# One router and one plan for the last four batches, and tile 0's loads moved into the attention

## Chip, cores and metric

The kernel runs on one core of one Trainium2 chip. The metric is the device time of one execution in microseconds (us), lower is better; of several runs the median counts.

## What is computed

A decoder layer on x of 16 batches of 128 tokens and 256 channels, in fp32, with three residual steps. Cut to what matters:

```
x = x + attn(layernorm(x))        # 16 heads, latent size 72, causal softmax, then out_w (1152 x 256)
x = x + sigmoid(layernorm(x)) * wkv(ctx)     # two scans over time per channel, from ctx alone
x = x + ffn(layernorm(x))
  logits = h @ router_w.T                    # 8 experts
  (w1, e1), (w2, e2) = top two experts of each token, masked softmax gates
  out = sum over experts e of w_e * (silu(h @ w_gate[e].T) * (h @ w_up[e].T)) @ w_down[e].T
```

2048 tokens each go to two of eight experts, whose hidden size is 512.

## The kernel before

**The order.** Every engine runs its own program, and all of them walk one list of steps, ORDER, which the function schedule (L60) writes at build time. Each step has a name and arguments: S, N, T, Y are scores, softmax, transposes of the probabilities and the mix with V for one unit; O projects a quarter of a batch's z; add adds it to x; bn, agg, rs, nmb, xn, tx are layer norm and its transposes; sig, x2 the gated second step; lg, lgc, r1, r2, ra, r3, rw, r4 the router; p1, p2, p3 the plan; lw and ltk load weights and token lists, lxg gathers rows; sw, tg, up, sh, dn are one tile of the expert layer. Each engine executes its part of a step in this order, and semaphores make it wait for the others.

**Attention.** 64 units (UNITS, L32), one for a batch and four heads. From unit 40 on the units of one batch follow each other. A unit's scores stand in step n, its N in n+1, its T and Y in n+3. In each unit of the loop (L365) there are five turns at which other work is taken in. Y's copy (copy_mixed, L1358) puts the mix into ZT, and SyncE packs it into zP by four DMAs (pack_z, L739). O of a batch (project, L912) reads zP.

**The planner.** The lists in beside (L282) hold generators that emit steps. At each turn (L289) a credit of st["share"] is added and the steps spend it; rest(n) (L72) puts a list to sleep for n times st["pace"] turns; users of the PSUM bank TR keep st["gap"] turns apart (L76). Before a value is needed, finish (L303) runs the generators without limits until a condition holds. stage_e (L266) is what follows the attention for a group of four batches (NG = 4): second norm, gate, x2, store of x, third norm, store of the rows to xd in HBM, their transposes, and the router. The last group is done in two halves, batches 12 and 13, then 14 and 15, each with a router and a plan of its own.

**Router and plan.** For each token the router finds two experts (choose_first L1438, choose_second L1447), counts ranks by matmuls (ranks, L949), makes slot numbers (slots, L1463) and weights (L1476), and GpSimd scatters number and weight of each token into xs in HBM (scatter_slots, L1713; one indirect DMA per batch and choice, 32 in all). A plan (L1490 to L1535) turns the counts of each expert into a list of tiles of 256 tokens: expert and first row of each go to PI, from which SyncE reads them into registers. PHASES gives how many tiles are sure after 12, 14 and 16 batches: tiles 0 to 4 come from plan 0, tiles 5 and 6 from plan 1, tiles 7 to 22 from plan 2. So tile 5 can't be loaded before batches 12 and 13 are routed.

**Tiles.** 23 tiles (NT). For a tile SyncE loads three blocks of an expert's weights (load_w, L761, 512 KB each) into WR[j % 2] and the token list into TK (load_tk, L776, which waits for all scatters that the phase needs). GpSimd gathers the rows from xd into XG[j % 4] (gather_rows, L1723), TensorE transposes them (transpose_rows, L960). Each fp32 operand is split into a high part (ScalarE, w_hi L1166, rows_hi L1179, hidden_hi L1190) and a low part (VectorE, w_lo L1537, rows_lo L1542, hidden_lo L1554), and each product is three matmuls (mm3, L811). gate_up (L971) runs twice for a tile, down (L990) once. ScalarE weighs the result into Y, and GpSimd adds it to out in HBM by two indirect DMAs (add_out, L1737), which wait until those of the tile before have landed.

**Where the change meets.** After the last Y, finish (L386) runs what is left of plan 0; then come the token lists, the weights of tiles 0 and 1, the gathers and the splits of tile 0 (L387 to L397), all still inside the unit loop, and the projections of batch 15 after them. WR[0] lies in the arena of the scans and is free when these end; WR[1], WF, GT, SG, HF, HR and Y lie over the attention's buffers (s1, L507 to L524). The tile loop (L414) has a turn (beside_turn, L405) between any two steps, seven in a tile, and emits loads up to three tiles ahead where the plan is there.

Functions that the diff touches:

## Time and profile before

| | us |
|---|---|
| median of 3 runs | 676.19 (672.5 to 677.79) |
| the profiled execution | 672.7 |
| its span | 671.0 |
| TensorE, VectorE, ScalarE, GpSimd busy | 559.1, 425.7, 368.8, 325.0 |
| mean granted TensorE clock | 0.944 of full speed |

The span runs from the first to the last instruction on the profile; the profiled execution's own time has 1.7 us around it. Rows below are from this one execution. Times in them are microseconds from the span's start. In the timeline, merged lines of one engine may cover several instructions (xN), "idle before" is how long the engine stood and what ended it.

### The profile page before, as it was taken

The numbers are of one execution on the slowest core, as the hardware profiler recorded it, in microseconds if no ns is written. First come the engines' busy times: TensorE is split into PE (matmuls) and PEld (weight loads), VectorE is DVE, ScalarE is ACT, GpSimd is POOL, SyncE is SP. The second block draws the span as 40 slices with busy tenths as digits, with TensorE's granted clock in tenths as the row PEclk, the third lists the DMA queues.
The fourth block names the chain that finished last, engine by engine and source line by source line (L and its number), as shares of the span: only waits on it lengthen the run. The fifth ranks groups of instructions, "written<-read, shape, count | busy, mean of one in ns | idle before, by whom it ended". The sixth has DMA issues, their size and how long they took to land.

```text
span 671.0 us, 11309 instructions
## 1 busy us (share of the span) xinstructions
PE 559.1 (83%) x3775; PEld 488.3 (73%) x3775; DVE 425.7 (63%) x942; ACT 368.8 (55%) x1000; POOL 325.0 (48%) x299
## 2 busy tenths in 40 slices
PE   1997869998979998999879725767889899999990
PEld 0885757776768876778657425667889899999990
DVE  4468475565876739755754617778877577777750
ACT  5276535755658545655554213655567567766750
POOL 3274635625254275621721531145546676666543
PEclk9999879999999998999999858879899899999996
DMA  6234444463434323624312145446379788888710
GB/s 234 78 55 66 54 65 73 61 89 53 65 82 98 51 42 56 103 73 62 49 60 59 36 162 203 137 105 165 88 235 248 202 211 239 219 222 226 171 30 0
DMA packets 55757, 75.92 MB, mean 113 GB/s; under 512 B 11730, under 2 KB 45140, under 8 KB 55444
## 3 DMA queue, kind: packets, MB, share of 16 engines
q1 hardware_dynamic: 45098, 64.90, 40.3%
q0 software_dynamic: 9856, 10.28, 8.3%
q8 instruction: 30, 0.49, 0.3%
q14 instruction: 27, 0.22, 0.1%
q10 hardware_dynamic: 746, 0.02, 0.1%
HBM read 48.90 MB, written 10.40 MB: 88 GB/s over the span
## 4 chain that ended last, share of the span: by engine, by line
PE 37%; DVE 21%; issue 11%; POOL 10%; DMA 9%; ACT 8%; SPq 2%; POOLq 0%; DVEq 0%; ACTq 0%
PE P L814 16%; PE PO L814 6%; PE PO L923 5%; ACT EB L1115 3%; DMA out<-Y,TK 3%; PE P L892 3%; PE P L910 2%; DVE ZT L1363 2%; DVE small L1352 2%; DVE arena L1385 2%; POOL EB L1684 2%; DMA zP<-ZT 2%; POOL xs L1720 2%; POOL out L1744 2%; DMA cxa<-xd,TK 2%
## 5 line engine op out<-in xcount | busy, mean ns | idle before, releaser
L1684 POOL TENSOR_TENSOR EB<-EB,small 128x512 f32<-128x512 f32 x64 | 75.9, 1187 | 158.6 <-DVE small L1356 158.5
L1115 ACT ACTIVATE EB<-P,small 128x128 f32<-128x128 f32 x256 | 90.3, 365 | 112.4 <-DVE small L1352 112.3
L814 PE MATMUL P<-GT,WF 128*128 128x256 f32 x1104 | 148.4, 293 | 3.2 <-DVE GT L1262 2.5
L814 PEld LDWEIGHTS P<-GT,WF 128*128 128x128 f32 x1104 | 141.5, 200 | 3.6 <-DVE GT L1262 2.7
L1744 POOL DMA_INDIRECT out<-Y,TK x46 | 83.7, 1820 | 63.7 <-DMA out<-Y,TK 36.1
L910 PE MATMUL P<-PT,V 128*72 128x512 f32 x128 | 69.1, 623 | 17.6 <-DVE ZT L1363 13.0
L1734 POOL DMA_INDIRECT cxa<-xd,TK x46 | 52.7, 1145 | 58.3 <-DMA TK<-xs 46.1
L892 PEld LDWEIGHTS P<-KT,qT 72*128 72x128 f32 x512 | 68.7, 196 | 11.6 <-DMA qT<-qP 8.2
L892 PE MATMUL P<-KT,qT 72*128 72x128 f32 x512 | 69.7, 280 | 7.1 <-DMA qT<-qP 6.7
L923 PE MATMUL PO<-Ow,zP 128*128 128x256 f32 x288 | 74.8, 401 | 0.0
L814 PE MATMUL PO<-WF,HR 128*128 128x256 f32 x552 | 70.1, 284 | 0.0
L1363 DVE COPY ZT<-P 72x512 f32<-72x512 f32 x64 | 43.0, 672 | 42.5 <-PE P L910 39.8
L814 PEld LDWEIGHTS PO<-WF,HR 128*128 128x128 f32 x552 | 68.0, 193 | 0.0
L1262 DVE TENSOR_TENSOR WF<-arena,WF 128x1024 fp32r<-128x1024 f32 x36 | 44.1, 1224 | 35.3 <-ACT WF L1177 35.3
L923 PEld LDWEIGHTS PO<-Ow,zP 128*128 128x128 f32 x288 | 54.1, 200 | 8.6 <-issue 0.2
L900 PEld LDWEIGHTS P<-ident,EB 128*128 128x128 f32 x256 | 33.0, 146 | 37.1 <-issue 32.4
L1352 DVE TENSOR_REDUCE small<-P 128x4 f32<-128x512 f32 x64 | 43.4, 677 | 23.1 <-PE P L892 23.0
L1262 DVE TENSOR_TENSOR WF<-WR,WF 128x1024 fp32r<-128x1024 f32 x33 | 40.4, 1224 | 21.0 <-ACT WF L1177 21.0
L1120 ACT ACTIVATE PT<-P 128x512 f32<-128x512 f32 x64 | 38.6, 603 | 25.7 <-PE P L900 25.5
L1115 ACT ACTIVATION_READ_ACCUMULATOR EB<-P,small 128x1 f32 x256 | 51.9, 203 | 0.0
L1177 ACT ACTIVATE WF<-arena 128x1024 fp32r<-128x1024 f32 x36 | 38.0, 1055 | 17.8 <-DMA arena<-wf 17.8
L1720 POOL DMA_INDIRECT xs<-TKS,SL x32 | 37.9, 1184 | 20.0 <-DVE TKS L1481 12.0
(187 smaller groups left out, 945.0 us busy)
## 6 DMA issues: line engine op xcount, KB each, us to landing
arena<-wf SPq DMA_DIRECT2D x36, 512.0 KB, 4.4
WR<-wf SPq DMA_DIRECT2D x33, 512.0 KB, 4.4
qT<-qP SPq DMA_DIRECT2D x63, 128.0 KB
zP<-ZT SPq DMA_DIRECT2D x80, 72.0 KB
zP<-ZT SPq DMA_DIRECT2D x96, 36.0 KB
X<-x SPq DMA_DIRECT2D x4, 512.0 KB, 6.0
cxa<-ctxin SPq DMA_DIRECT2D x4, 512.0 KB, 6.5
out<-X SPq DMA_DIRECT2D x3, 512.0 KB, 3.8
```

What stands on the lines that cost most here:

```text
L814: r = e.matmul(o, lt(a), rt_(b), start=start and n == 0, stop=stop and n == 2, skip_group_check=skip)
L892: p = e.matmul(S[:, 128 * j:128 * j + 128], qT[k % 2][:, 4 * hq + j, c:c + 128], KT[g % 2][:, r:r + 128], start=False, stop=True, skip_gro ...
L910: e.matmul(YB[0:L, :], V[g % 2][:, b % GB, :], PT[n % 2][:, :], start=True, stop=True).then_inc(s_Y, 1)
L923: p = e.matmul(o, zP[b // NB % 2][:, m, 128 * (b % NB):128 * (b % NB) + 128], Ow[:, m, :], start=False, stop=m == NQ - 1)
L1115: e.activation(EB[i][:, j, :], S[:, 128 * j:128 * j + 128], ACT.Exp, bias=NM[i][:, j:j + 1], accum_out=SM[i][:, j:j + 1]).then_inc(s_exp, 1)
L1262: return e.tensor_tensor(o, src, hi.bitcast(fp32), ALU.subtract)
L1352: e.tensor_reduce(NM[n % 3], SB[n % 2][:, :].rearrange("p (h s) -> p h s", h=4), AX.X, ALU.max, negate=True).then_inc(s_max, 1)
L1363: e.tensor_copy(ZT[z % 2][:, :, c:c + 128], YB[0:L, :].rearrange("p (h t) -> p h t", h=4)).then_inc(s_z, 1)
L1684: e.tensor_tensor(EB[i][:, :, :], EB[i][:, :, :], SM[i].unsqueeze(2).broadcast_to([128, 4, 128]), ALU.mult).then_inc(s_prob, 1)
L1720: e.indirect_dma_start(xs, bass.IndirectOffsetOnAxis(ap=SL[:, g, c, b:b + 1], axis=0), TKS[:, g, c, b, :], None).then_inc(s_sc[g + b0 // 2 ...
L1734: e.indirect_dma_start(XG[i][:, a_, :], None, xd[0:(TN * 3 // 4, TN * 7 // 8, TN + 1)[phase(j)], :], bass.IndirectOffsetOnAxis(ap=TK[:, j, ...
L1744: e.indirect_dma_start(outr, bass.IndirectOffsetOnAxis(ap=TK[:, j, a_, 0:1].bitcast(i32), axis=0), Y[j % 2][:, a_, :], None, bounds_check= ...
```

## The change

- The last group's two halves share one router and one plan: PHASES has two entries (tiles 0 to 4 after 12 batches, 5 to 22 after 16), the router of batches 12 to 15 runs when batch 15's third norm is done, and the scatters of the last group count on one semaphore.
- From unit 52 on (LATE) the planner's share is 0.9, its pace 0.6 and the gap 3; in the tiles share, pace and gap are 3, 0.5 and 3 (before 4, 0.1, 3).
- A generator lists stands behind plan 0 and emits the weight loads of tile 0 and the first three token lists during the attention, where SyncE also packs z.
- The first half of the last group gets a list of its own that starts at unit 62.
- After the loop: gathers, splits and transposes of tile 0, weights of tile 1, up(0,0), and only then the projections of batch 15 and the last add.
- Ow, Lw and the bias rows move behind zP in SBUF and no longer lie under HR and Y; w_hi(0) waits for the queries, w_hi(1) for the mixes, where both waited for projections.
- If the plan of the next tile isn't there at the end of a tile, finish runs then, before the next tile's splits; before, it ran at the tile's start.

The diff, without the lines that only rename:

```diff
 NT = (2 * TN + NE * (TW - 1)) // TW
-PHASES = [-(-(2 * n - NE * (TW - 1)) // TW) for n in (TN * 3 // 4, TN * 7 // 8)] + [NT]
+PHASES = [-(-(2 * (TN * 3 // 4) - NE * (TW - 1)) // TW), NT]
 NX = 4
-SHARE, SHARE_TILES = 0.7, 4.0
-GAP, GAP_TILES = 5, 3
-PACE, PACE_TILES = 1.0, 0.1
+SHARE, SHARE_TILES = 0.7, 3.0
+GAP, GAP_LATE, GAP_TILES = 5, 3, 3
+PACE, PACE_TILES = 1.0, 0.5
+LATE, SHARE_LATE, PACE_LATE = 52, 0.9, 0.6
 SCANS_FROM = 0
...
         if g == NG - 1:
-            yield from plan(1 + b0 // 2)
+            yield from plan(1)
...
         yield from own(e_ln3(g, b0, nb), "norm")
-        yield from own(e_route(g, b0, nb), "route")
+        if b0 + nb == GB:
+            yield from own(e_route(g, 0, GB), "route")
...
+    def lists():
...
+        yield from rest(5)
+        for k in range(3):
+            load_w(0, k)
+        yield from rest(3)
+        for j in range(3):
+            emit("ltk", j)
...
+    waiting = []
...
+    def load_w(j, k):
+        if j < NT:
+            if phase(j) in planned:
+                emit("lw", j, k)
+            else:
+                waiting.append((j, k))
...
+    def split_w(j, k):
+        if j < NT:
+            emit("sw", j, k)
+            load_w(j + 2, k)
...
     beside = [[(0, first()), (0, stage_a(1)), (0, own(ln1_stats(2), "norm")), (0, own(ln1_stats(3), "norm")), (19, stage_a(2)), (35, stage_a(3))],
               [(27, stage_e(0, 0, GB)), (43, stage_e(1, 0, GB)),
-               (54, stage_e(2, 0, GB)), (54, plan(0)), (62, stage_e(3, 0, 2))],
-              [(NU + 4, stage_e(3, 2, 2))],
+               (54, stage_e(2, 0, GB)), (54, plan(0)), (54, lists())],
+              [(62, stage_e(3, 0, 2)), (NU + 3, stage_e(3, 2, 2))],
               [(SCANS_FROM, scans(g, k)) for g in range(NG) for k in range(2)],
...
             if b >= NB * PAIRED:
-                at_i = at + (4 + i // 2 if b < B - 1 else 3)
+                at_i = at + 4 + i // 2
             else:
...
                 at_i = at + 5 + (i // fast if b % 2 == 0 else 4 // fast + (i // 2 if b % 4 == 3 else i // fast))
-            o_steps.setdefault(at_i, []).append((b, i))
+            if b < B - 1:
+                o_steps.setdefault(at_i, []).append((b, i))
...
-    waiting = []
...
-    def load_w(j, k):
-        if j < NT:
-            if phase(j) in planned:
-                emit("lw", j, k)
-            else:
-                waiting.append((j, k))
...
-    def split_w(j, k):
-        if j < NT:
-            emit("sw", j, k)
-            load_w(j + 2, k)
...
-    for n in range(NU + 4):
+    def projections_of(b):
+        for i in range(4):
+            emit("O", b, i)
...
+    for n in range(NU + 3):
+        if n == LATE:
+            st.update(gap=GAP_LATE, share=SHARE_LATE, pace=PACE_LATE)
         if 3 <= n < NU + 3:
...
         turn(n)
-        if n == NU + 2:
-            finish(n, lambda: 0 in planned and NG - 1 in w_done)
-            for j in range(3):
-                emit("ltk", j)
-            for k in range(3):
-                load_w(0, k)
-            for k in range(3):
-                load_w(1, k)
-            for j in range(3):
-                emit("lxg", j)
-            split_w(0, 0)
-            split_w(0, 1)
-            emit("tg", 0)
+    finish(n, lambda: ("ltk", 2) in order and NG - 1 in w_done)
+    for j in range(3):
+        emit("lxg", j)
+    split_w(0, 0)
+    split_w(0, 1)
+    emit("tg", 0)
+    for k in range(3):
+        load_w(1, k)
+    emit("up", 0, 0)
+    projections_of(B - 1)
+    emit("add", NK - 1)
...
     def beside_turn(upto):
-        turn(NU + 4)
+        turn(NU + 3)
         while waiting and ready(waiting[0][0]):
...
     for j in range(NT):
-        if j + 1 < NT and not ready(j + 1):
-            finish(NU + 4, lambda: ready(j + 1))
+        due = j + 1 < NT and not ready(j + 1)
...
+        def prepare(k):
+            if not due:
+                split_w(j + 1, k)
...
         beside_turn(j + 3)
-        split_w(j + 1, 0)
-        emit("up", j, 0)
+        prepare(0)
+        if j:
+            emit("up", j, 0)
         beside_turn(j + 3)
-        if j + 1 < NT:
+        if j + 1 < NT and not due:
             emit("tg", j + 1)
         beside_turn(j + 3)
-        split_w(j + 1, 1)
+        prepare(1)
         emit("sh", j, 0)
...
         beside_turn(j + 3)
+        if due:
+            finish(NU + 3, lambda: ready(j + 1))
+            beside_turn(j + 3)
+            split_w(j + 1, 0)
+            emit("tg", j + 1)
+            split_w(j + 1, 1)
     emit("dn", NT - 1)
...
         qT = [sb(f"qT{i}", [L, H, 128 * NB], fp32, s1) for i in range(2)]
+        EB = [sb(f"EB{i}", [128, 4, 128], fp32, s1) for i in range(3)]
+        PT = [sb(f"PT{i}", [128, 512], fp32, s1) for i in range(2)]
+        ZT = [sb(f"ZT{i}", [L, 4, 128 * NB], fp32, s1) for i in range(2)]
+        maskr = sb("maskr", [128, 4, 128], f32r, s1)
+        identr = sb("identr", [128, 128], f32r, s1)
+        zP = [sb(f"zP{i}", [128, NQ, 128 * NB], fp32, s1) for i in range(2)]
         Ow = sb("Ow", [128, NQ, C], fp32, s1)
...
         onr = sb("onr", [1, 128], f32r, s1)
-        EB = [sb(f"EB{i}", [128, 4, 128], fp32, s1) for i in range(3)]
-        PT = [sb(f"PT{i}", [128, 512], fp32, s1) for i in range(2)]
-        ZT = [sb(f"ZT{i}", [L, 4, 128 * NB], fp32, s1) for i in range(2)]
-        zP = [sb(f"zP{i}", [128, NQ, 128 * NB], fp32, s1) for i in range(2)]
-        maskr = sb("maskr", [128, 4, 128], f32r, s1)
-        identr = sb("identr", [128, 128], f32r, s1)
         s1.close()
...
                 if q == 0:
-                    pe.wait_ge(s_xt3, xt_count("tx", 3, g, b0, nb, 1))
+                    pe.wait_ge(s_xt3, xt_count("tx", 3, g, 0, GB, 1) if g < NG - 1 else xt_count("tx", 3, g, 2, 2, 1))
                     tr_wait("lg", g, b0, nb, q)
...
                 ac.wait_ge(s_wf[i][k], 16 * (j // 2 + 1))
-                if j == 0 and k < 2:
+                if j == 0:
                     ac.wait_ge(s_q, total["q"])
-                elif j < 2:
-                    ac.wait_ge(s_O, 4 * B)
+                elif j == 1:
+                    ac.wait_ge(s_Y, NU)
                 elif k == 2:
```

## Rows read from the trace of the kernel before

**Rows 1.** Windows of the last units, the drain, tiles 0 to 4 and the steady tiles

```profile
core 0: us, PE busy (x) PEld busy (x) DVE busy (x) ACT busy (x) POOL busy (x), PEclk, DMA share, GB/s
330.00:383.00 53.00, 45.61 (x228) 33.76 (x228) 28.33 (x93) 23.38 (x86) 19.90 (x20) 0.90 0.18 49
383.00:398.00 15.00, 0.29 (x2) 0.02 (x1) 2.99 (x14) 0.36 (x1) 6.08 (x7) 0.64 0.29 85
398.00:473.00 75.00, 53.77 (x364) 50.83 (x365) 55.94 (x181) 39.74 (x62) 22.24 (x18) 0.85 0.55 167
...
528.00:656.00 128.00, 127.70 (x1060) 127.50 (x1058) 88.94 (x107) 86.42 (x136) 79.28 (x53) 0.99 0.72 185
```

**Rows 2.** Chain of waits: start us, us, what

```profile
388.55 0.67 SPq L748
...
399.82 6.26 PE PO L923 x18
...
592.62 0.44 PE P L968 x4
...
635.11 2.88 PE P L814 x24
```

**Rows 3.** Timeline, last units to tile 0: start us, us, engine, line, op

```profile
349.44 1.90 PE L910 MATMUL P<-PT,V 128*72 128x512 f32 x2 [3.84 <-ACT PT L1120]
...
374.02 1.04 POOL L1684 TENSOR_TENSOR EB<-EB,small 128x512 f32<-128x512 f32 x1 [2.58 <-DVE small L1356]
...
382.19 1.08 PE L910 MATMUL P<-PT,V 128*72 128x512 f32 x2 [0.69 <-ACT PT L1120]
...
385.69 0.69 DVE L1363 COPY ZT<-P 72x512 f32<-72x512 f32 x1
...
392.45 0.99 POOL L1734 DMA_INDIRECT cxa<-xd,TK  x1 [7.40 <-DMA TK<-xs]
...
397.98 1.12 PE L968 MATMUL P<-ident,cxa 128*128 128x128 f32 x4 [14.71 <-DMA cxa<-xd,TK]
...
405.72 3.22 PE L814 MATMUL P<-GT,WF 128*128 128x256 f32 x24
...
406.11 0.69 DVE L1368 TENSOR_TENSOR X<-PO,X 128x512 f32<-128x512 f32 x1 [1.03 <-PE PO L923]
```

**Rows 4.** Timeline in tiles 1 to 4: batches 12, 13 and 14, 15

```profile
421.76 0.69 PE L832 MATMUL P<-ident,XN 128*128 128x128 f32 x2 [9.53 <-ACT XN L1076]
...
427.04 0.75 DVE L1293 BATCH_NORM_STATS2 small<-X 128x6 f32<-128x256 f32 x2
...
445.83 0.17 DVE L1470 TENSOR_TENSOR small<-P,small 128x16 f32<-128x16 f32 x1
...
472.66 0.17 DVE L1470 TENSOR_TENSOR small<-P,small 128x16 f32<-128x16 f32 x1
```

**Rows 5.** Waits of TensorE from 380 to 528: us in total, times, longest

```profile
PE P L968 <- DMA cxa<-xd,TK: 19.6, 3, 14.7
...
PE P L832 <- ACT XN L1076: 13.0, 2, 9.5
```

**Rows 6.** Timeline, tiles 5, 7 and 10 transposed, and scatters between

```profile
472.65 0.60 PE L968 MATMUL P<-ident,cxa 128*128 128x128 f32 x4
...
474.88 1.00 POOL L1720 DMA_INDIRECT xs<-TKS,SL  x1 [5.20 <-DVE TKS L1481]
...
482.00 2.05 POOL L1720 DMA_INDIRECT xs<-TKS,SL  x1 [0.30 <-issue]
...
484.35 2.02 POOL L1720 DMA_INDIRECT xs<-TKS,SL  x1 [0.30 <-issue]
...
497.60 0.66 PE L968 MATMUL P<-ident,cxa 128*128 128x128 f32 x4 [2.39 <-DMA cxa<-xd,TK]
...
527.63 1.11 PE L968 MATMUL P<-ident,cxa 128*128 128x128 f32 x4 [2.45 <-DMA cxa<-xd,TK]
```

**Rows 7.** Timeline, the last matmuls

```profile
649.78 5.92 PE L814 MATMUL PO<-WF,HR 128*128 128x256 f32 x48
```

More of the change, by code:

```diff
@@ L636, in build @@
         s_xd = [sem(f"xd_stored{i}") for i in range(5)]
-        s_sc = [sem(f"slots_scattered{i}") for i in range(5)]
+        s_sc = [sem(f"slots_scattered{i}") for i in range(NG)]
         s_out = [sem(f"x2_stored{i}") for i in range(5)]
@@ L778, in load_tk @@
                 for i in range(3 + phase(j)):
-                    sp.wait_ge(s_sc[i], SCATTERS[i])
+                    sp.wait_ge(s_sc[i], SCATTERS)
                 sp.wait_ge(s_fill, 48)
@@ L801, in sync_program @@
             sp.wait_ge(s_acc, 32 * NT)
+            for i in range(NG):
+                sp.wait_ge(s_sc[i], SCATTERS)
             for i in range(5):
-                sp.wait_ge(s_sc[i], SCATTERS[i])
                 sp.wait_ge(s_out[i], 16)
@@ L1491, in plan_counts @@
                 j0, n, nf, tl, te, one, first, m, v, eid, rs, un, tmp = plan_views(i)
-                second = i == 2
+                second = i == 1
                 ve_.wait_ge(s_run, 3 + i)
@@ L1505, in plan_tiles @@
                 j0, n, nf, tl, te, one, first, m, v, eid, rs, un, tmp = plan_views(i)
-                second = i == 2
+                second = i == 1
                 cmp, jb = big[0:1, 0:n, :], jio[0:1, 0:n]
@@ L1720, in scatter_slots @@
                     e.indirect_dma_start(xs, bass.IndirectOffsetOnAxis(ap=SL[:, g, c, b:b + 1], axis=0),
-                                         TKS[:, g, c, b, :], None).then_inc(s_sc[g + b0 // 2], 16)
+                                         TKS[:, g, c, b, :], None).then_inc(s_sc[g], 16)
             def gather_rows(j):
@@ L1725, in gather_rows @@
                 po.wait_ge(s_tk[j % 4], 16 * (j // 4 + 1))
-                for d in range(3 + phase(j)):
+                for d in range(5 if phase(j) else 3):
                     po.wait_ge(s_xd[d], 16)
@@ L1733, in gather_rows @@
                 for a_ in range(2):
-                    e.indirect_dma_start(XG[i][:, a_, :], None, xd[0:(TN * 3 // 4, TN * 7 // 8, TN + 1)[phase(j)], :],
+                    e.indirect_dma_start(XG[i][:, a_, :], None, xd[0:(TN * 3 // 4, TN + 1)[phase(j)], :],
                                          bass.IndirectOffsetOnAxis(ap=TK[:, j, a_, 0:1].bitcast(i32), axis=0)).then_inc(s_xg[i], 16)
@@ L1772, in build @@
         PARTS = ((0, 1024), (1024, 2048), (2048, 3072))
-        SCATTERS = [16 * 8, 16 * 8, 16 * 8, 16 * 4, 16 * 4]
+        SCATTERS = 16 * 2 * GB
         block = ctx.enter_context(nc.Block())
```

## The prediction

> **What bounds the kernel now.** I read the table of windows first. Outside the tail it has four stretches [rows 1]. In the last attention units TensorE is busy 45.61 of 53.00 us. From 383 to 398 it is busy 0.29 of 15.00. From 398 to 473, tiles 0 to 4, it is busy 53.77 of 75.00 at a granted clock of 0.85 of full speed, while VectorE is at 55.94. From 528 on it is busy 127.70 of 128.00. So TensorE bounds the later tiles and nothing in the diff makes those cheaper: three groups of 24 matmuls at 2.88 us and four transposes at 0.44 [rows 2] make 9.08 us a tile. The time to be won lies between the last unit and about tile 10.
>
> Then I followed the chain of waits and the timeline through that stretch. At its start the last z copy ends at 386.39 behind the plan's own VectorE instructions [rows 3], its packing is issued until 389.22 [rows 2], the token list comes only then, the first gather is issued at 392.45 and lands at 397.98, where tile 0 is transposed [rows 3]. The last output projection takes 6.26 us [rows 2], x1 is added at 406.11 and up(0,0) runs from 405.72 to 408.94 [rows 3]. In the middle, TensorE stands at the normalised rows of batches 12 and 13 for 9.53 us [rows 4], and the list of waits has 13.0 us in two such waits and 19.6 us in three waits for gathered rows [rows 5]. At its end tile 7, the first of the last plan, is transposed at 497.60, and tile 10 at 527.63 [rows 6].
>
> A yardstick: from the transposes of tile j to the last matmul there are 22-j tiles and then six groups, (22-j) x 9.08 + 17.7 us. From tile 5 (472.65) this gives 644.7, and the last matmul ends at 655.70 [rows 6, 7]: 11.0 us are lost after tile 5, most of them to the second plan. The tail from there to the span's end is 15.3 us. The profiled execution took 672.7 for a span of 671.0, so 1.7 is added to a span. It is 3.5 under the median of 676.19, near the fastest of the three; I return to that at the end.
>
> **Where the order moves things.** From unit 52 on the planner gives 0.9 instead of 0.7 of credit per turn and rests 0.6 as long. Walking its turns (five per unit), group 2 has its logits in unit 59 (62 before), slots at 60, p1 and p2 at 61, p3 at the start of 62 (end of 66 before). The three weight loads of tile 0 fall in unit 63, the three token lists two turns later. Batches 12 and 13 start their second norm in unit 62 and have their third norm transposed by unit 66; all that stood in tiles 0 and 1 before. In the tile phase a tile has seven turns. Counted from the first one (share 3, pace 0.5, gap 3), batches 14 and 15 have statistics in turn 1, x2 in 4, third norm in 6 and 7, transposes in 10 and 13, logits in 16, slots in 19, scatters in 19 to 22, plan in 23 and 24, which is tile 3's third turn. So tile 5's plan stands in the order before it is due, and the forced finish is empty.
>
> **Attention's end.** The moved plan is 5.1 us of small VectorE instructions, and two passes of statistics of 3.3 us each join units 62 to 66. Where such a pass sits in a unit now, TensorE waits 3.84 us for the copied probabilities and the unit takes longer at 349.44 [rows 3]. Against it, the plan no longer holds back the last z copy (2.4 us: the mix ends at 383.27, its copy starts at 385.69). SyncE gets six loads with register reads between packings, 7.5 us of its queue (389.43 to 397), and the packings of units 60 to 63 stand behind it; TensorE has up(0,0) to run meanwhile. Bounds of the net shift of the last z copy: 2.4 earlier, 6 later. I take 1.6 later, 388.0.
>
> **Tile 0 at once.** GpSimd has nothing after the last probabilities (374.02 before, [rows 3]) but gathers, so tile 0's rows land by 384, and w_hi/w_lo(0) run in the drain. The transposes of tile 0 wait for that z copy: 388.0 + 1.1 + the split of the rows (0.6 on ScalarE, 0.7 on VectorE) = 390.4. up(0,0) takes 3.2 and hides the last packing. O of batch 15 is 6.3 at the lower clock, 18 of its matmuls at 0.35 us each [rows 2]; the clock had fallen after TensorE had stood from 383.27 on, and as that stand is now some 2 us, I take 4.8, most of the matmuls at full clock (in the windows the clock was 0.64 of full speed over that stand, [rows 1]), with 7.0 as the other bound. With 0.7 for the add and some issue time the statistics of batch 14 start at 399.7.
>
> **One router.** The second chain before went from its statistics at 427.04 to its slots at 472.66, 45.6 us; the first from the end of the add, 406.80, to 445.83, 39.0 [rows 4]. The new one has about as many turns, but half of the routing beside it is gone: one set of choices (3.1 us), slots and weights (1.5) and a plan (4.6), 9 us of VectorE in the stretch where VectorE is the fuller engine. My walk through its in-order queue with these durations (7.1 us of splits and products a tile) gives 37.5. Ends 35 and 50; I take 40, nearest to the first chain. TensorE still stops once at the transposes of the normalised rows, now those of 14 and 15. Slots start at 439.7, weights are there at 441.1.
>
> **Scatters, list, gather.** Before, the last group had four scatters left; now it has eight, with one pair of output adds between them. Four at 1.27 (0.97 and the 0.3 between), 4.3 for the adds, four at about 1.8 (between 1.27 and the 2.35 of those at 482.00 and 484.35 with the 0.3, [rows 6]) are 16.5: 441.9 to 458.4. From the last scatter's end (486.37) to the transposes of its first tile (497.60) it took 11.2. So tile 5 is transposed at 469.6, against 472.65 before. TensorE could be there at about 455: some 14 us of standing, which before were spent on tiles 5 and 6 from the middle plan.
>
> **The rest.** From 469.6 the yardstick gives 641.7. Of the 11.0 us lost after tile 5 the half that belongs to the second plan goes (tiles 5 to 22 now have one plan and two lists are fetched at once); a cold restart and late output adds remain, and 3 us are kept, with 1 and 7 as bounds. Last matmul 644.7, span 660.0, time 661.7: 11 us less than the profiled 672.7. The gain is 3 us at tile 5 and 8 behind it. As medians lie a little over a profiled execution, the forecast for the median is 662.5, 2.0% under 676.19. The other moves (buffers of the attention laid out anew, waits on counts of Y for those of O) take or add no instruction on the path and are put at nothing; the new layout is what lets O of batch 15 run behind up(0,0), and without it the add would be 3 us sooner and tile 0 later by 5.
>
> **Rivals.** (a) The chain is freer than that: with 35 us to the slots and scatters at 1.27, tile 5 comes at 463 and the time is near 655. For it: half the routing, a warm clock. Against: both chains before needed 39 and more.
> (b) All scatters are slow. A scatter lasts 0.97 us beside a quiet VectorE and 2.02 to 2.05 beside its busy spell at 482 [rows 6]. Eight of these with the adds are 22.9 instead of 16.5, so 668 to 669. The Trainium skill, SBUF — State Buffer, section "Who interferes with whom", says that a VectorE instruction with two SBUF inputs blocks a GpSimd one that reads SBUF, and whoever comes second waits. By that rule every scatter of the tile phase is at risk; the trace agrees only for some of them.
> (c) Slower: TensorE starves at tile 5. The single plan is the only source of tiles behind tile 4, and nothing covers its lateness. With the second chain's 45.6, the slow scatters and a list that lands as late as the slowest scatter's (7 us more), tile 5 comes at 399.7 + 45.6 + 2.2 + 22.9 + 18.2 = 488.6 and the time is 681. It decides from tile 5 at 484.
> (d) The head start doesn't come: VectorE and SyncE, packed denser from unit 52 on, stretch the last units by 10 us or more, and tile 0 starts hardly sooner; 672 to 676.
>
> **How the numbers follow.** The forecast 0.50, (a) 0.20, (b) 0.13, (c) 0.07, (d) 0.10. Three runs of before span 5 us, so about 1% is what a measurement tells from no change; 1% under the median is 669.4. Faster takes (a), nearly all of the forecast and half of (b): 0.74. Within 1%: the rest of (b), a little of the forecast and most of (d): 0.18. Slower: (c) and what is left, 0.08. The range leaves out (c) and the far side of (a): 648 to 674.
>
> **What would show it.** In the profile after: tile 0 transposed near 389 and not 398; the last add by 400; TensorE busy between 385 and 395; one chain of choices in the tiles; eight scatters in a row near 442 to 458; one long wait of TensorE at the transposes of tile 5, for gathered rows, about 14 us; from some 478 on no waits. It is wrong if the last z copy is past 394, if tile 5 comes later than 476 or earlier than 463, or if TensorE stands again behind tile 6.

## The result, and the profile after

| | before | after |
|---|---|---|
| median, us | 675.25 (670.41 to 682.86, 20 runs) | 669.53 (666.04 to 673.01, 20 runs) |
| ratio, 95% interval | | 0.9925 (0.9898 to 0.9951) |
| span of the profiled execution | 671.0 | 665.0 |

Faster by 0.75%, where 2.0% was forecast: the right sign, inside the range, well under half the gain. The ratio is taken over all fast runs and not from the two medians, whose quotient is 0.9915; further down, too, the two can differ by 0.2%.

The windows after, with the columns of [rows 1]:

```profile
330.00:383.00 53.00, 40.32 (x204) 30.40 (x204) 35.41 (x130) 24.62 (x94) 20.43 (x20) 0.89 0.17 48
383.00:398.00 15.00, 9.97 (x38) 6.73 (x38) 5.24 (x20) 4.84 (x8) 7.27 (x8) 0.84 0.69 214
398.00:473.00 75.00, 50.81 (x359) 48.44 (x359) 47.52 (x123) 33.39 (x51) 22.89 (x19) 0.86 0.51 134
473.00:528.00 55.00, 50.73 (x408) 50.73 (x409) 35.28 (x42) 34.71 (x55) 37.43 (x25) 0.92 0.81 217
528.00:656.00 128.00, 123.55 (x1035) 123.34 (x1033) 87.21 (x106) 84.37 (x133) 79.93 (x51) 1.00 0.70 182
```

Read the first two together. TensorE is now busy for 9.97 us between 383 and 398, where it had 0.29, but not with tile 0: that is attention, which it didn't do between 330 and 383 (40.32 busy against 45.61) while VectorE had 7 us more. The drain wasn't filled with new work; the attention slid into it.

The timeline after, at the places that the prediction named (start us, us, engine, line, operation, idle before and releaser):

```profile
378.25 0.68 DVE L1380 TENSOR_REDUCE small<-P 128x4 f32<-128x512 f32 x1
...
387.98 0.69 DVE L1391 COPY ZT<-P 72x512 f32<-72x512 f32 x1 [1.03 <-PE P L938]
393.77 0.69 DVE L1391 COPY ZT<-P 72x512 f32<-72x512 f32 x1 [5.11 <-issue]
397.09 0.69 DVE L1391 COPY ZT<-P 72x512 f32<-72x512 f32 x1 [2.62 <-DMA zP<-ZT]
...
397.92 1.08 PE L996 MATMUL P<-ident,cxa 128*128 128x128 f32 x4 [2.26 <-DVE ZT L1391]
400.70 4.36 PE L842 MATMUL P<-GT,WF 128*128 128x256 f32 x24 [1.69 <-DVE GT L1290]
...
405.41 4.15 PE L951 MATMUL PO<-Ow,zP 128*128 128x256 f32 x18
...
409.60 0.69 DVE L1396 TENSOR_TENSOR X<-PO,X 128x512 f32<-128x512 f32 x1 [3.75 <-PE PO L951]
...
448.04 0.18 DVE L1498 TENSOR_TENSOR small<-P,small 128x32 f32<-128x32 f32 x1
...
477.27 1.11 PE L996 MATMUL P<-ident,cxa 128*128 128x128 f32 x4 [15.85 <-DMA cxa<-xd,TK]
...
645.63 5.92 PE L842 MATMUL PO<-WF,HR 128*128 128x256 f32 x48
```

The last z copy ends at 397.78 (386.38 before, 388.0 forecast). Tile 0 is transposed at 397.92, in the same place as in [rows 3] but for another reason: it stood behind a gather before, and stands behind that copy now. The last add comes at 409.60, 3.5 us later than in [rows 3].

TensorE's waits after, from 380 to 528 (total, times, longest):

```profile
PE P L996 <- DMA cxa<-xd,TK: 15.9, 1, 15.9
PE P L842 <- DVE GT L1290: 6.0, 2, 4.4
PE P L860 <- ACT XN L1104: 5.1, 1, 5.1
PE PO L949 <- DMA zP<-ZT: 3.1, 1, 3.1
PE P L938 <- DVE ZT L1391: 2.8, 1, 2.8
```

Beside [rows 5]: one long wait for gathered rows where there were three, and 5.1 us of waiting for normalised rows where there were 13.0. From 478 on the list of waits is empty. New are the waits for zP and ZT, which belong to the attention's end.

SyncE's own queue after, from 377 on (start, us from first to last issue, count):

```profile
377.90 2.82 SPq L775 DMA_DIRECT2D zP<-ZT  x4
382.10 2.67 SPq L801 DMA_DIRECT2D arena<-wf  x3
385.68 2.55 SPq L811 DMA_DIRECT2D TK<-xs  x3
388.27 2.92 SPq L775 DMA_DIRECT2D zP<-ZT  x4
...
391.74 2.85 SPq L775 DMA_DIRECT2D zP<-ZT  x4
...
395.14 5.85 SPq L775 DMA_DIRECT2D zP<-ZT  x8
```

The six loads stand between 382.10 and 388.23. The z copy that ended at 382.77 is packed only from 388.27, and a z copy needs the packing of the copy two before it to have landed. So the z copies at 393.77 and 397.09 stand 5.11 and 2.62 us; the profile names the releaser (<-DMA zP<-ZT) for the second and writes "issue" at the first.

### The profile page after: what moved, and what is told of

Its sections match the earlier page's. It is cut to its first block, busy times and chain, and to the rows that moved or that the text cites. A ratio compares the mean times of both kernels' runs of the same rounds, so it can differ in the third digit from the quotient of the medians.

```text
span 665.0 us, 11259 instructions
## 1 busy us (share of the span) xinstructions
PE 558.7 (84%) x3778; PEld 489.2 (74%) x3778; DVE 418.1 (63%) x888; ACT 366.6 (55%) x997; POOL 328.6 (49%) x300
## 3 DMA queue, kind: packets, MB, share of 16 engines
q1 hardware_dynamic: 45098, 64.90, 39.5%
## 4 chain that ended last, share of the span: by engine, by line
PE 45%; DVE 20%; issue 12%; POOL 10%; ACT 7%; DMA 4%; another core or an unknown queue 1%; SPq 0%; POOLq 0%; ACTq 0%; DVEq 0%
PE P L842 22%; PE PO L842 9%; PE PO L951 4%; DVE ZT L1391 3%; ACT EB L1143 3%; PE P L920 3%; DVE small L1380 2%; POOL EB L1712 2%; POOL xs L1748 2%; DVE arena L1413 2%; PE P L938 2%; DVE arena L1415 2%; DMA qT<-qP 1%; PE P L996 1%; DMA arena<-wd 1%
## 5 line engine op out<-in xcount | busy, mean ns | idle before, releaser
L1772 POOL DMA_INDIRECT out<-Y,TK x46 | 74.5, 1619 | 53.5 <-ACT Y L1229 43.5
L1762 POOL DMA_INDIRECT cxa<-xd,TK x46 | 64.2, 1396 | 60.3 <-DMA TK<-xs 51.5
L920 PEld LDWEIGHTS P<-KT,qT 72*128 72x128 f32 x512 | 70.6, 201 | 9.3 <-DMA qT<-qP 5.8
L920 PE MATMUL P<-KT,qT 72*128 72x128 f32 x512 | 71.3, 284 | 5.0 <-DMA qT<-qP 4.6
L1290 DVE TENSOR_TENSOR WF<-arena,WF 128x1024 fp32r<-128x1024 f32 x36 | 43.9, 1221 | 20.9 <-ACT WF L1205 20.6
L1748 POOL DMA_INDIRECT xs<-TKS,SL x32 | 38.3, 1195 | 21.9 <-DVE TKS L1509 13.8
L1221 ACT ACTIVATE HR<-HF 128x512 fp32r<-128x512 f32 x46 | 28.9, 628 | 22.0 <-DVE HF L1580 20.4
```

What stands on the lines that cost most here:

```text
L920: p = e.matmul(S[:, 128 * j:128 * j + 128], qT[k % 2][:, 4 * hq + j, c:c + 128], KT[g % 2][:, r:r + 128], start=False, stop=True, skip_gro ...
L1290: return e.tensor_tensor(o, src, hi.bitcast(fp32), ALU.subtract)
L1748: e.indirect_dma_start(xs, bass.IndirectOffsetOnAxis(ap=SL[:, g, c, b:b + 1], axis=0), TKS[:, g, c, b, :], None).then_inc(s_sc[g], 16)
L1762: e.indirect_dma_start(XG[i][:, a_, :], None, xd[0:(TN * 3 // 4, TN + 1)[phase(j)], :], bass.IndirectOffsetOnAxis(ap=TK[:, j, a_, 0:1].bit ...
L1772: e.indirect_dma_start(outr, bass.IndirectOffsetOnAxis(ap=TK[:, j, a_, 0:1].bitcast(i32), axis=0), Y[j % 2][:, a_, :], None, bounds_check= ...
```

## Experiments

Four sets of runs, each set one job on one chip beside the kernel before; the four chips differ. I measure two stretches: U, ten units long, from the row max of unit 53 to that of unit 63 (the last), and Z, from that row max to the end of the last z copy. (The expectations of set 4 say unit 52; the times in them start at the row max of unit 53, which is the eleventh from the end.) Before, U is 50.60 us and Z 16.85; after, 60.96 and 19.53. The median of the kernel before is 675.50 in set 1, 673.54 in set 2, 675.41 in set 3 and 674.58 in set 4.

**Set 1: one part of the change at a time.**

lists_late: weights of tile 0 and token lists emitted behind the loop again.

```diff
-               (54, stage_e(2, 0, GB)), (54, plan(0)), (54, lists())],
+               (54, stage_e(2, 0, GB)), (54, plan(0))],
...
-    finish(n, lambda: ("ltk", 2) in order and NG - 1 in w_done)
+    finish(n, lambda: 0 in planned and NG - 1 in w_done)
+    for j in range(3):
+        emit("ltk", j)
+    for k in range(3):
+        load_w(0, k)
```

> The changed kernel with its three token lists and three weight loads of tile 0 put back behind the last Y, all else as changed. Two causes are weighed for the last z copy, which ends at 397.8 instead of the forecast 388.0. Theory P (the denser planner from unit 52 on): the last row maximum stays at about 378 and the last z copy ends at 394 to 395, as only the two waits for packing (5.1 and 2.6 us) go. Theory Q (SyncE's queue): most of the delay goes, last z copy by 391. In both, tile 0's rows are late: gathers at about 400, tile 0 transposed near 406 by P, 402 by Q. Time: P 676 to 678, Q 671 to 673 (changed kernel 669.5).

Measured: 676.13, ratio 1.0012 (0.9986 to 1.0037). The last row max stands at 375.24 and the last z copy ends at 391.31, between the two theories; the time is P's. Z falls to 16.1, and yet tile 0 is transposed only at 403.85, after 13.3 us of waiting for its rows. So whatever the early lists cost the z copies, they pay: without them nothing is left of the gain.

calm_planner: the planner's setting as before to the end of the attention.

```diff
-LATE, SHARE_LATE, PACE_LATE = 52, 0.9, 0.6
+LATE, SHARE_LATE, PACE_LATE = 99, 0.9, 0.6
```

> The changed kernel with LATE = 99, so share, pace and gap of the units stay 0.7, 1.0 and 5 to the end. The plan comes as late as before, and the lists behind the last Y by themselves. P: the last row maximum is back at 370 (378 in the changed kernel), the last z copy ends by 388; tile 0 transposed near 399; the router of the last group is a tile later, so tile 5 is transposed at 484 to 488 and the time is 675 to 679. Q: the last row maximum stays past 375, the z copy at 392 or later. If earliness of the plan was worth nothing, the time is 666 or less.

Measured: 685.53, ratio 1.0146 (1.0102 to 1.0189). U is back at 51.3, with the last row max at 369.59 as before, as theory P has it. But plan 0 isn't there when the loop ends: tile 0 comes at 408.84 (399 expected) after 23.3 us of waiting for rows, tile 5 at 498.00 after another 18.9, and the time lies past the 675 to 679 expected. The dense packing costs time in the units, and the rest of the change needs it.

loads_spread: the same six loads, one at a time between packings.

```diff
-        yield from rest(5)
-        for k in range(3):
-            load_w(0, k)
-        yield from rest(3)
-        for j in range(3):
-            emit("ltk", j)
+        yield -1
+        load_w(0, 0)
+        yield -4
+        load_w(0, 1)
+        yield -4
+        emit("ltk", 0)
+        yield -4
+        emit("ltk", 1)
+        yield -3
+        load_w(0, 2)
+        emit("ltk", 2)
```

> The changed kernel with the same six SyncE loads spread over units 62 to 66 (weights 0, weights 1, list 0, list 1, then weights 2 and list 2) instead of in two bunches in unit 62 and 63. P: the last row maximum stays at 378; the waits of the last two z copies for packing shrink from 7.7 to under 3 us, the last z copy ends near 395, everything behind it moves with it: 666 to 667.5. Q: up to 8 us earlier, 662 to 664. If the waits for packing are no cost at all: 669 to 670.

Measured: 665.61, ratio 0.984 (0.98 to 0.9881). The z copies no longer wait for a packing:

```profile
384.00 0.69 DVE L1396 COPY ZT<-P 72x512 f32<-72x512 f32 x1 [1.65 <-PE P L943]
387.24 0.69 DVE L1396 COPY ZT<-P 72x512 f32<-72x512 f32 x1 [2.56 <-PE P L943]
389.66 0.69 DVE L1396 COPY ZT<-P 72x512 f32<-72x512 f32 x1 [1.73 <-PE P L943]
```

Their releaser is TensorE's mix; Z is 16.7, 3 us shorter than with the loads in a bunch. U remains 56.6: that part has another cause. Both theories missed: the last z copy ends at 390.35 (395 by P), and the time is 0.4 us under P's range.

router_alone: the kernel before with only the merge of the last two routers and plans (the PHASES, router, plan, semaphore and gather lines of the change).

```diff
-            yield from plan(1 + b0 // 2)
+            yield from plan(1)
...
-        yield from own(e_route(g, b0, nb), "route")
+        if b0 + nb == GB:
+            yield from own(e_route(g, 0, GB), "route")
```

> The kernel before with one router and one plan for batches 12 to 15 and nothing else of the change. Starvation (the single plan is the only source of tiles 5 and up): tile 0 transposed at 398 as before, tile 5 at 486 to 492 after a wait of more than 18 us, later tiles without waits, time 679 to 683, slower than before. Rival: the 9 us of VectorE work that fall away shorten the chain enough, tile 5 by 478, time 668 to 672.

Measured: 685.94, ratio 1.0138 (1.0088 to 1.0188). TensorE's waits from 380 to 528:

```profile
PE P L970 <- DMA cxa<-xd,TK: 36.1, 2, 21.9
PE P L834 <- ACT XN L1078: 19.4, 2, 9.8
```

Against [rows 5], waiting for gathered rows rises from 19.6 to 36.1 us, and 21.9 of it stand ahead of tile 5, which comes at 495.48 (486 to 492 expected). The time is 3 us past the range given for starvation. The merge by itself costs some 10 us: the VectorE work that it saves is worth less than the two tiles that the middle plan gave TensorE meanwhile.

**Set 2: the parts taken on from the changed kernel.**

changed_again: the changed kernel, unchanged.

> The changed kernel itself, beside the same runs of the kernel before as the next three: ratio 0.990 to 0.995, last z copy within 3 us of 397.8.

Measured: 665.28, ratio 0.9874 (0.984 to 0.9908), a larger gain than in the result above and than expected. U is 56.6, Z 20.0, with two z copies waiting 4.82 and 3.36 us for packings. Tile 0 is transposed at 394.21, 3.8 us sooner than in the kernel before. I return to the difference in sets 3 and 4.

short_queue: three of the six loads between packings, three after the loop.

```diff
-        yield from rest(5)
-        for k in range(3):
-            load_w(0, k)
-        yield from rest(3)
-        for j in range(3):
-            emit("ltk", j)
+        yield -1
+        load_w(0, 0)
+        yield -4
+        load_w(0, 1)
+        yield -4
+        emit("ltk", 0)
...
-    finish(n, lambda: ("ltk", 2) in order and NG - 1 in w_done)
+    finish(n, lambda: ("ltk", 0) in order and NG - 1 in w_done)
+    emit("ltk", 1)
+    load_w(0, 2)
+    emit("ltk", 2)
```

> As loads_spread, but of the six SyncE loads only weights 0, weights 1 and list 0 stand in units 62 to 64; list 1, weights 2 and list 2 stand behind the last packing. In loads_spread the last packing was issued until 397.9 although its z was copied by 390.4, and O of batch 15 waited 2.4 us for it at the lower clock (7.0 us for 18 matmuls); only 1.8 of the 7.4 us won at the last z copy reached the last add. Queue theory: the packing is issued until 395, O of batch 15 runs at 397, the last add at 403 to 405 (407.9 in loads_spread), tile 5 3 us earlier, 661 to 663. If the add is not bound by the queue: 665 to 666.

Measured: 664.09, ratio 0.9841 (0.9809 to 0.9873). The time lies between the two theories. Z is 16.3, 3.7 us under changed_again's, but the last add comes at 407.52 against 406.24 there, and the intervals of the two ratios overlap. loads_spread says the same: its 665.61 is no less than changed_again's 665.28 (the ratios, 0.984 and 0.9874, overlap too), and its last packing is issued until 397.86, against 397.25 in changed_again. The bunched loads hold back the z copies; that they cost the kernel time isn't shown.

two_routers_again: short_queue with two routers and three plans, as before the change (the two halves of the last group stand in two lists again).

```diff
-        if b0 + nb == GB:
-            yield from own(e_route(g, 0, GB), "route")
+        yield from own(e_route(g, b0, nb), "route")
...
-               (54, stage_e(2, 0, GB)), (54, plan(0)), (54, lists())],
-              [(62, stage_e(3, 0, 2)), (NU + 3, stage_e(3, 2, 2))],
+               (54, stage_e(2, 0, GB)), (54, plan(0)), (54, lists())],
+              [(NU + 3, stage_e(3, 2, 2))],
+              [(62, stage_e(3, 0, 2))],
```

> short_queue with the two routers and plans of the kernel before (tiles 5 and 6 from the plan behind batch 13), all else as changed. Starvation theory: the wait of 15.7 us before tile 5 goes, though VectorE has some 9 us more; tile 5 is transposed at 464 to 470, tile 7 waits less than 4 us, and the time is 653 to 659. VectorE theory (the one router pays by what VectorE no longer does): the chain takes 9 us more and tile 7 waits as tile 5 did; 664 to 670.

Measured: 651.27 (650.25 to 652.25), ratio 0.9656 (0.9626 to 0.9687), 13 us under short_queue and 2 under the starvation theory's range. Tiles 5, 6 and 7 are transposed at

```profile
462.87 0.60 PE L998 MATMUL P<-ident,cxa 128*128 128x128 f32 x4
...
471.94 0.60 PE L998 MATMUL P<-ident,cxa 128*128 128x128 f32 x4
...
481.01 0.60 PE L998 MATMUL P<-ident,cxa 128*128 128x128 f32 x4
```

without a wait, 9.07 us apart, the price of a tile in the prediction. No wait for gathered rows is left from 380 to 528, and TensorE is busy for 55.00 of the 55 us from 473 on. With one router, in the run of the result, it had 50.73.

add_first: short_queue with O of batch 15 and its add ahead of up(0,0).

```diff
-    emit("up", 0, 0)
...
+    emit("up", 0, 0)
```

> short_queue with O of batch 15 and the last add ahead of up(0,0) in the order. If the chain from the last add alone sets tile 5, and TensorE has time before it: the add comes 0 to 2 us earlier and the time is the same or up to 2 us less than short_queue's. If up(0,0) hides the packing and its own place matters: 2 to 4 us more.

Measured: 663.64, ratio 0.9844 (0.9811 to 0.9877), the same as short_queue. The add comes at 403.02 instead of 407.52 and tile 5 at 473.58 instead of 476.92, but the profiled execution of short_queue was its slowest (666.43), with U at 58.3 against 56.6. In the medians nothing of it is seen: which of the two goes first doesn't matter here.

**Set 3: what stretches the units.**

two_routers_bunched: the changed kernel with only the merge undone (the part of two_routers_again's diff on routers, plans and lists), its loads bunched as they were.

> The changed kernel with only the merge of the last two routers undone: two routers, three plans, the lists and weights bunched exactly as in the change. Theory A (one router starves TensorE at tile 5, because all four lists come only after the last batch's sums): the wait of some 16 us at tile 5 is gone and the tiles' first list-dependent waits with it, time 652 to 655, about 13 us under the changed kernel; the last z copy stays late, 393 to 398. Rival B (the merge pays through the VectorE work it saves, and the gain of the earlier variant came from the spread loads): time 664 or more.

Measured: 660.07, ratio 0.9777 (0.9733 to 0.982), 9.5 us under the changed kernel's 669.53, which stems from another job. Less than the 13 forecast and no lower than 660, but tile 5 comes at 470.39 with no wait for rows. The gain of the two routers isn't that of the spread loads.

dense_alone: the kernel before with the dense setting alone.

```diff
+        if n == 52:
+            st.update(gap=3, share=0.9, pace=0.6)
```

> The kernel before with the planner's dense setting alone (share 0.9, pace 0.6, gap 3) from unit 52 on; routers, plans and loads as before. Theory A (it is the dense packing of VectorE and GpSimd work into the last units, not the merged router or the loads, that stretches them): the last row max comes at 374 to 377 where the kernel before has it at 369.5 and the kernels with the calm planner at 369.6 and 370.7. Time 660 to 672, since the third group's plan no longer stands in the middle of the tiles. Rival B (the merged work or the early loads stretch the units): last row max 369 to 371.

Measured: 669.61, ratio 0.9916 (0.9882 to 0.995), as good as the whole change. The last row max comes at 379.68, past the 374 to 377 expected: U is 62.7. Tile 0 is transposed at 408.26, 10 us later than before, and the kernel gains all the same: the slots of batches 12 and 13 are there at 416.53 instead of 445.83 [rows 4], and TensorE's list of waits from 466 on has no gathered or normalised rows in it.

share_seven: two_routers_again with share 0.7 in the last units, pace and gap kept.

```diff
-LATE, SHARE_LATE, PACE_LATE = 52, 0.9, 0.6
+LATE, SHARE_LATE, PACE_LATE = 52, 0.7, 0.6
```

> The version with two routers and spread loads, with share 0.7 in place of 0.9 in the last units, pace and gap kept. Theory A (the share is what stretches the units): last row max back at 370 to 372, but some of the third group's plan falls behind the loop; time 650 to 656. Rival B (the pace or the gap, or the amount of work as such, stretches them): row max at 374 to 378 all the same, time within 2 us of 651.3.

Measured: 665.67, ratio 0.9865 (0.9818 to 0.9912). U is 60.6 though VectorE has only 34.9 us in it. The last row max at 378.12 is near rival B's 374 to 378, the time far from the 649 to 656 of both theories. The plans fall behind the loop, and the units aren't shorter.

best_try: two_routers_again with add_first's order and the dense setting from unit 54 on.

> The version with two routers and spread loads, with the output projection of batch 15 and its add ahead of the first up projection, and the dense planner from unit 54 on instead of 52. Theory A (the bunched scatters of group 1 in units 52 to 54 stretch one unit by some 5 us, and the dense planner put them there): units 52 to 54 take 4 to 5 us each, the last row max falls at or below 374, time 648 to 651. Rival B (the work that those units give up is done in later units at the same price): row max 374 to 378, time within 1 us of 651.3.

Measured: 656.06, ratio 0.9717 (0.9676 to 0.9759), last row max 381.83: a miss for both theories.

In this set every kernel but dense_alone was slower than expected, and every U long. The table of U says why that isn't the kernels' doing alone:

| | U, us | VectorE busy in it |
|---|---|---|
| calm setting: before, calm_planner, router_alone | 50.6, 51.3, 52.5 | 29.9 |
| dense, sets 1 and 2 (six profiles) | 56.6 to 58.3 | 39.3 to 39.5 |
| dense, the run of the result and set 3 (five) | 60.6 to 63.6 | 34.9 to 39.4 |

That the dense setting stretches the units is shown twice: calm_planner, the changed kernel without it, has 51.3, and dense_alone, the kernel before with it alone, has 62.7. The list of waits over U points at VectorE (ScalarE for VectorE's row max in before, calm_planner and changed_again, and TensorE for VectorE's z copy, in changed_again alone):

```profile
ACT EB L1115 <- DVE small L1352: 10.0, 8, 1.7
ACT EB L1143 <- DVE small L1380: 10.2, 8, 1.9
ACT EB L1143 <- DVE small L1380: 18.1, 10, 5.0
PE P L938 <- DVE ZT L1391: 6.2, 3, 2.9
```

GpSimd has 26.8 us of work in U where it had 21.0, and the units pass through it too; its part isn't separated from VectorE's.

The changed kernel is in both dense rows. Its VectorE in the run of the result, at the start of the stretch:

```profile
317.29 0.69 DVE L1380 TENSOR_REDUCE small<-P 128x4 f32<-128x512 f32 x1 [0.88 <-PE P L920]
...
320.56 0.69 DVE L1396 TENSOR_TENSOR X<-PO,X 128x512 f32<-128x512 f32 x1 [2.49 <-issue]
322.69 0.69 DVE L1391 COPY ZT<-P 72x512 f32<-72x512 f32 x1 [1.45 <-remote]
326.62 0.69 DVE L1380 TENSOR_REDUCE small<-P 128x4 f32<-128x512 f32 x1 [3.24 <-remote]
```

and in changed_again:

```profile
317.49 0.69 DVE L1380 TENSOR_REDUCE small<-P 128x4 f32<-128x512 f32 x1 [0.88 <-PE P L920]
...
319.22 0.69 DVE L1396 TENSOR_TENSOR X<-PO,X 128x512 f32<-128x512 f32 x1 [0.95 <-PE PO L951]
320.08 0.69 DVE L1391 COPY ZT<-P 72x512 f32<-72x512 f32 x1 [0.17 <-PE P L938]
321.64 0.69 DVE L1380 TENSOR_REDUCE small<-P 128x4 f32<-128x512 f32 x1 [0.88 <-PE P L920]
```

From the first row max to the next it takes 9.3 us in the one and 4.2 in the other. In the short one each has a releaser among the engines; in the long one the idle time is put down to "issue" or "remote", which names none. ScalarE has such idle times there too (3.89 us at 323.41, ahead of a copy whose transposes had ended at 320.27), and again 3.76 us at 371.52. The label alone proves little: the z copy at 393.77 above has "issue" and waited for a DMA. The delay itself is what differs.

**Set 4: the job or the kernel?** The cause was still open, so four kernels were run in one job, on a fourth chip.

> The changed kernel itself, with the three kernels beside it in one job. Its two profiles so far have units 52 to 63 (row max of unit 52 to that of unit 63) in 60.96 us, with idle times of VectorE and ScalarE around 320 to 327 for which the profile shows no releaser, and in 56.58 us without these. Theory A (the unexplained idle times belong to the job, the packing to the kernel): all dense kernels of this job agree with each other, either all with such idle times near 320 and 60 to 63 us, or all without and 56 to 58. Rival B (they fall by chance in each execution, or belong to the kernel's layout): they differ within the job.

Measured: 669.16, ratio 0.9926 (0.9896 to 0.9955). U is 64.7, VectorE's row max stands at 326.46 with 4.70 us before it and no releaser.

> Two routers and spread loads, unchanged, beside best_try's kernel. If the jobs differ and not the kernels, this one and the next agree within 2 us here, though they stood at 651.3 and 656.1 in two jobs; if the dense setting from unit 52 on instead of 54 is what is better, this one is 3 to 6 us faster.

Measured: 656.44, ratio 0.9733 (0.9686 to 0.978), U 61.5.

> The version with the dense setting from unit 54 on and the last add first. If jobs differ and not kernels: within 2 us of the version before it, ratio to the kernel before 0.963 to 0.970 if no unexplained idle times show, 0.970 to 0.975 if they do.

Measured: 654.71, ratio 0.9718 (0.9674 to 0.9762), U 63.6. The two agree within 2 us; starting at unit 54 is neither better nor worse.

> The kernel before with the dense setting alone. Theory A: its units 52 to 63 take 56 to 58 us if the changed kernel of this job has 56 to 58, against some 51 for the kernel before, so that the packing by itself costs 5 to 7 us and the unexplained idle times the rest. Rival B: 60 us or more here too, so that the packing costs 10 or more by itself. Time within 2 us of the changed kernel's in either case.

Measured: 666.54, ratio 0.9915 (0.9884 to 0.9946), U 60.7, and 2.6 us under the changed kernel, a little more than the 2 expected.

All four are long and all four have idle times of 2 to 5.4 us with no releaser between 321 and 329, so theory A holds, with a longer upper end than I gave it. They go with the job, and as every set had a chip of its own, job and chip can't be told apart: none of this length in sets 1 and 2, in every profile of sets 3 and 4 but one. The exception is best_try, whose longest is 1.42 us (at 330.16) and whose U is 63.6 all the same, so these idle times aren't the whole of the difference. Dense packing costs 5 to 7 us in the units of sets 1 and 2 (56.6 to 58.3 against about 51.5) and 9 to 13 in the others. What the idle times are, no profile here says, and no calm kernel was profiled in sets 3 and 4. The kernel before has medians of 673.5 to 675.5 in the result and all four sets, so it doesn't seem to suffer from them.

## Why the prediction failed

**The step that failed is "Attention's end".** It put the last z copy 1.6 us later, at 388.0, with bounds of 2.4 earlier and 6 later. It came 11.4 later, in two parts: the last row max 8.7 later (U longer by 10.4, less 1.6 for an earlier start) and Z longer by 2.7. The prediction had listed the causes: 5.1 us of plan and two passes of statistics of 3.3 put into units 62 to 66, and six loads ahead of the packings in SyncE's queue. No sum leads from there to the 1.6: nearly all of these 5.1, 6.6 and 7.5 us were put at nothing, without a row that says what they would hide behind. What could have hidden them is VectorE's idle time (28.33 busy of 53.00 in [rows 1]) and up(0,0), and VectorE's idle time covers only a part. A unit is a chain that passes from TensorE to VectorE, ScalarE, GpSimd and back, and much of VectorE's idle time is where it waits its turn in the chain. In changed_again VectorE has 9.5 us more work in U than before, ScalarE waits 8.1 us longer for VectorE's row max, TensorE stands 6.2 us at its z copies, and the stretch is 6.0 us longer. In the run of the result it is 10.4 us longer; the cause of the other 4.4 stays open (set 4). I also looked only at units 62 to 66, and the dense setting begins at 52.

The SyncE term had its mechanism right: z copies wait for packings that stand behind the six loads. Its size is some 3 us in Z, as far as Z tells: 19.3 to 20.6 in the four profiles of dense kernels with bunched loads, 16.1 to 18.6 in ten of the eleven without; but calm_planner and router_alone, with no loads there, have 20.0 and 19.5, so Z moves by that much for other reasons too. Against it I had set a gain of 2.4 for the moved plan; without the loads Z is 16.1 in lists_late against 16.85 before, under 1 us less, with the passes of statistics in it.

**Rival (d), the head start that doesn't come, is what happened to the start**: the units stretched by 10.4 us, its condition was "10 us or more", and tile 0 is transposed where it was. It had a chance of 0.10. Its time, 672 to 676, was too high, as the steps behind tile 0 gained most of what was forecast for them. In changed_again, with U 6.0 us longer, the head start did come, 3.8 us of the 9 forecast.

**From the z copy on the steps held.** From the copy's end to up(0,0) it took 2.9 us (2.4 forecast). O of batch 15 took 4.15 us (4.8 forecast), but its warm clock came otherwise than forecast: the granted clock was 0.50 of full speed from 397.9 to 400.7, 0.68 over up(0,0), which therefore took 4.36 us instead of 3.2, and 1.00 over O. up(0,0) paid for the cold clock that O had paid before; the two together took 8.5 us, 8.0 forecast. From the copy to the statistics it took 12.6 us against 11.7.

The chain to the slots took 37.7 (40 forecast, my walk gave 37.5). One of the two lengths that the 40 was taken from was misread: the first chain doesn't start behind the add of 406.11, which is that of batches 14 and 15. Its own statistics stand before that add:

```profile
403.84 0.75 DVE L1293 BATCH_NORM_STATS2 small<-X 128x6 f32<-128x256 f32 x2
```

So it took 42.0 us, not 39.0, and 40 was below both chains; that the new one came out at 37.7 bears out the walk and not the comparison. First to last scatter took 16.1 against 16.5, and tile 5 came 10.7 after the last (11.2). TensorE stood 15.85 us ahead of it ("some 14"). Tile 5 came at 477.27 instead of 469.6: the 9.8 us of the first step, less some 2 won in the chain. It lies past the 476 that I named as the mark of being wrong, and the z copy past its 394.

**The rest.** Behind tile 5 the yardstick gives 649.3 for the last matmul and it ends at 651.55: 2.2 us lost, 3 forecast. The tail took 13.45 instead of 15.3. So 9.8 late at the start, less 2.1 up to tile 5, 0.8 behind it and 1.9 in the tail, is the 5 us between the forecast span of 660.0 and the 665.0 measured. The other 2 us of the miss are the median's: it lies 2.8 us over the profiled execution, where 0.8 was allowed.

**Rival (b), slow scatters,** came in small part. The eight scatters after:

```profile
450.44 1.16 POOL L1748 DMA_INDIRECT xs<-TKS,SL  x1 [9.87 <-DVE TKS L1509]
451.90 1.42 POOL L1748 DMA_INDIRECT xs<-TKS,SL  x1 [0.30 <-issue]
453.62 0.96 POOL L1748 DMA_INDIRECT xs<-TKS,SL  x1 [0.30 <-issue]
454.89 0.96 POOL L1748 DMA_INDIRECT xs<-TKS,SL  x1 [0.31 <-issue]
...
459.96 1.18 POOL L1748 DMA_INDIRECT xs<-TKS,SL  x1 [0.30 <-issue]
461.45 2.02 POOL L1748 DMA_INDIRECT xs<-TKS,SL  x1 [0.30 <-issue]
463.77 1.53 POOL L1748 DMA_INDIRECT xs<-TKS,SL  x1 [0.30 <-issue]
465.61 0.96 POOL L1748 DMA_INDIRECT xs<-TKS,SL  x1 [0.30 <-issue]
```

The three of 0.96 us fall where VectorE has the small instructions of the plan (453.00 to 455.94) or stands (after 465.06). The five longer ones, 1.16 to 2.02, all overlap its splits of weights or hidden values, as 1.21 us from 460.80 and 1.23 from 463.24. The rule of the Trainium skill, SBUF — State Buffer, section "Who interferes with whom", is that a VectorE instruction with two SBUF inputs contends with a GpSimd one that reads SBUF; this trace agrees for the five scatters and not for the output add between them, which overlaps a split from 458.46 on and takes 1.58 us like the others. The overlaps cost less than rival (b) had it because three scatters fell in quiet stretches and two more were lengthened by only 0.2 us.

**Rival (c), starvation at tile 5,** didn't decide the sign, but it is what the change pays most for. I had booked "some 14 us of standing" as no loss, since those tiles were fed from the middle plan before. Undoing the merge is worth 13 us in set 2 and, across two jobs, 9.5 in set 3. By single parts, the dense setting alone gains some 6 to 8 us, the early lists some 9 to 12 (lists_late against changed_again and loads_spread), and the merge costs 10 to 13; the change nets 5 to 8. The parts needn't add up: inside the change the dense setting is worth 20 us (calm_planner against changed_again). The version with two routers and spread loads beats both kernels in either job: 651.3 against 673.5 before and 665.3 changed in set 2, 656.4 against 674.6 and 669.2 in set 4.

## What to carry to other kernels

Idle time on an engine covers new work only if nothing behind it waits for that engine next. In a chain that hops between engines much of the idle time is the hop itself. Here 9.5 us of VectorE work (and 5.8 of GpSimd's) made the stretch 6 us longer at the least, so price inserted work at over half its length until a run says otherwise, and count it over the whole stretch that is packed, not only where the moved step lands. When two plans or stages are merged, ask what fed the bottleneck engine in between: work saved on another engine was worth less here than the two tiles of TensorE work that went missing. And repeat a result in a second job before explaining a difference of under 1%.

## What was not expected of the hardware

The same kernel has two ratios, 0.9874 in one job and 0.9925 and 0.9926 in two others, while the kernel before keeps its median within 2 us. With the larger ones VectorE and ScalarE stand idle for up to 4.7 us at a time between 320 and 327 with no releaser in the profile, and the ten units of U are 4 to 8 us longer. The sets ran on four chips, so whether it is the job or the chip is open. TensorE's granted clock over the stretch follows: 0.93 of full speed in changed_again, 0.86 in the run of the result and 0.82 in changed_third.
